# Opening stage of a four-layer vision network on one core: whole-row loads, relative positions by raster rows, key bias on chip, and paced expert weights

## The chip, the cores and the metric

The kernel runs on 1 core of a Trainium2 chip, in one launch. The time is device microseconds, the median of 3 runs. TensorE (PE) multiplies matrices into PSUM banks, VectorE (DVE), ScalarE (ACT) and GpSimd (POOL) do elementwise work, and SyncE (SP) mostly issues DMA transfers. The engines run side by side and wait for each other by semaphores.

## The reference, cut to what matters

The network has a window-attention block with an MLP, a Fourier block, a landmark attention, a two-expert layer, a full attention and a one-expert layer. Two places are touched: the front of the first block, and the last layer.

```python
h = _ln(x, norm1_w, norm1_b)             # x: 8 images of 16 x 16 tokens, 192 channels
win = windows(pad(h), 14)                # 14 x 14 windows; the real tokens give pieces of 14x14, 14x2, 2x14, 2x2
q, k, v = split(win @ qkv_w + qkv_b)     # 12 heads of 16 channels
attn = einsum('bqc,bkc->bqk', q * scale, k)
rel_h = einsum('bhwc,hkc->bhwk', q, rel_pos_h[h - k + 13])   # one small table for each row h of a window
rel_w = einsum('bhwc,wkc->bhwk', q, rel_pos_w[w - k + 13])   # and one for each column w
attn = softmax(attn + rel_h + rel_w)
...
h = gelu(expert_inputs[e] @ w1[e] + b1[e])           # last layer: 8 experts of 256 slots
expert_outputs[e] = gelu(h @ w2[e] + b2[e])
```

A padded token of a window has the key `qkv_b` alone (the key bias), and the kernel needs that bias times the scale as three bf16 pieces whose sum is the fp32 value. Queries, keys and relative positions are split in the same way (`Pieces`: ACT makes the first piece at L252, DVE the rest at L264, ACT the second piece at L268, POOL the third at L272, SP stores them).

## The kernel before

Each engine has its own program, written out by hand in the order in which it runs; a stage ends when all engines meet. Two stages matter here.

**The opening, `opening` (L307 to L602).** It has two parts.

- The image loop, one image of 256 tokens after another. DVE takes the statistics (L154, L157) and normalizes (L182); PE turns the result (L192); ACT scales it by the norm weights on its way out of PSUM (L203, L204). PE projects queries and keys (L438) and values (L445, every other image also L453). ACT copies q and k out (L505), and both go through `Pieces` to DRAM. DVE adds the value bias (L585, L589). Tokens of an image stand in window order: 14x14 first, then the three border pieces.
- Four rounds of `relative` (L455 to L466), for two channel halves by two axes. In each round PE multiplies the queries of one window row (or column) with that row's table, 32 matmuls into five PSUM banks: four banks for the 14x14 piece with 112 columns a row, and the fifth for all border pieces (16 or 112 columns a row). ACT empties banks 0 and 2, DVE banks 1, 3 and 4 (`evacuate_rel`), into RHW. Then RHW goes through `Pieces` in two halves, three DMAs a half, to the DRAM tensor rd. Three buffers of pieces take turns.

The order on SP's queue: loads of x, the qkv weights W, biases, the two relative tables RT as twelve transposing loads of 4-byte elements (L370), the key bias pieces to DRAM (L373, after ACT and DVE made them from `qkb`), a zero fill and constants, a wait until the key bias has landed, six loads that spread it over 96 partitions (L379), then the stores of q and k image by image, twelve loads of the first attention group (L913), and the rd stores (L281). On ACT's queue: the identity, norm weights, biases, convolution taps and a reversed identity, each as a transposing load of 4-byte elements except the identities. PE's first work is the reversal of the taps (L470), then 12 warm-up matmuls on the identity (L473).

**The last layer, `experts_each` (L2716) with `AllExperts` (L2685).** POOL gathers each expert's tokens (L2748), then 16 gate columns (L2752), then scatters results (L2757) and gathers the tokens of expert e+4. PE turns the tokens (L2784), computes six groups of hidden units for two experts (L2798, L2801), turns the next two experts' tokens and computes both results (L2812). ACT applies gelu (L2838, L2846); DVE adds the bias (L2873) and combines (L2883). Before `experts_each` SP keeps the rows in xn and loads the weights of experts 0 and 1; at its start, after PE's second turn, it issues the weights of experts 2 and 3, a store of all rows to `out`, and the weights of experts 4 to 7, without further waits. POOL's first scatter waits for that store.

Of the kernel before, what the change touches and what calls it, by code (L numbers as in the profile page):

```python
# [17 lines left out]
T = HH * WW  # L18
# [288 lines left out]
def opening(nc, G, x, w, w_conv, consts):  # L307

    with Stage(nc, "l0q") as st:
# [6 lines left out]
        taps, rev, backwards = st.sb("taps", [TAPS, NH]), st.sb("rev", [TAPS, TAPS]), st.sb("backwards", [NH, TAPS])  # L316
        wn, bn, qkb, kb4 = st.sb("wn", [CH, 2]), st.sb("bn", [CH, 2]), st.sb("qkb", [CH, 6]), st.sb("kb4", [CH, 2])
        kbp, kbr, kb = st.sb("kbp", [CH, 3, 2], BF16), st.sb("kbr", [CH, 2]), st.sb("kb", [SR, NH], BF16)
# [8 lines left out]
        ident_in, w_in, b_in, vb_in, tables_in, taps_in, band_out, first_in, kb_in, kb_out = st.sems("ident_in w_in b_in vb_in tables_in taps_in band_out first_in kb_in kb_out")  # L327
        rev_mm, rev_done, q_mm, q_free, k_mm, k_free, v_mm, v_free, e_free = st.sems("rev_mm rev_done q_mm q_free k_mm k_free v_mm v_free e_free")
        kb_step, kf_free, v_init, rbd_done, ones_done, pads_done = st.sems("kb_step kf_free v_init rbd_done ones_done pads_done")
        ps = [psE, nm.psT[0], nm.psT[1], psQ, psK]  # L330
        full, emptied = [st.sem(f"full{c}") for c in range(5)], [st.sem(f"emptied{c}") for c in range(5)]
# [3 lines left out]
        def fills(axis):  # L335

            first, *rest = runs(axis)
            out = [[(0, first, i0, min(4, WS - i0))] for i0 in range(0, WS, 4)]
            col, last = 0, []
            for run in rest:  # L340
                last.append((col, run, 0, run[0]))
                col += run[0] * B * run[3]
            return out + [last]

        def evacuate_rel(copy, bank, axis):
            for col, (n, base, si, cnt, step, su), i0, ni in fills(axis)[bank]:
                src = ps[bank][0:ROWS, col:col + ni * B * cnt].rearrange("p (i b u c) -> p i b u c", i=ni, b=B // 2, u=2)
                for u in range(2):
                    dst = RHW[:, axis, base + si * i0 + u * su:base + si * i0 + u * su + 1]
                    ins = copy(free(dst, [si, ni], [2 * T, B // 2], [step, cnt]), src[:, :, :, u])  # L350
            return ins
# [5 lines left out]
        def _(sp):  # L357
# [8 lines left out]
            sp.dma_start(vb[:, :], rows(w["qkv_b"], 2 * C, [0, P], [1, C])).then_inc(vb_in, 16)  # L366
            sp.dma_start(pb[:, :], rows(w["proj_b"], 0, [0, P], [1, C])).then_inc(vb_in, 16)
            for k, table in enumerate((w["rel_pos_h"], w["rel_pos_w"])):
                for hh in range(HB):
                    sp.dma_start(RT[hh * HD:(hh + 1) * HD, k, :], rows(table, 0, [1, HD], [HD, 2 * WS - 1]), allow_slow_non_contiguous=True).then_inc(tables_in, 16)  # L370
            sp.dma_start(hm[:, :], consts["headmask"]).then_inc(tables_in, 16)
            sp.wait_ge(kb_step, 5)
            sp.dma_start(rows(G["kbd"], 0, [1, CH], [2 * CH, 3], [CH, 2]), kbp[:, :, :], allow_slow_non_contiguous=True).then_inc(kb_out, 16)  # L373
# [3 lines left out]
            sp.wait_ge(kb_out, 16)  # L377
            for t, piece in enumerate(K_TERM):
                sp.dma_start(kb[t * HD:(t + 1) * HD, :], rows(G["kbd"], piece * C, [1, HD], [HD, NH]), allow_slow_non_contiguous=True).then_inc(kb_in, 16)  # L379
            for i in range(B):  # L380
                for pieces, dst in ((qp, G["qd"]), (kp, G["kd"])):
                    pieces.sync(sp, rows(dst, i // 2 * 3 * C * 2 * T + i % 2 * T, [2 * T, CH], [2 * C * T, 3], [2 * CH * T, 2], [1, T]), i, i % 2)
                if i == 0:
# [12 lines left out]
            sp.wait_ge(first_in, 16 * 14)  # L396
# [3 lines left out]
        def _(pool):  # L400
# [19 lines left out]
            for r, a, axis in rounds:  # L420
# [6 lines left out]
        def _(pe):  # L427
# [28 lines left out]
            def relative(r, a, axis):  # L456
                for bank, fill in enumerate(fills(axis)):
                    if r:
                        pe.wait_ge(emptied[bank], r)
                    else:  # L460
                        pe.wait_ge(*((e_free, B // 2), (nm.xT_done, B + 2), (nm.xT_done, B + 2), (q_free, B), (k_free, B))[bank])
                    for col, (n, base, si, cnt, step, su), i0, ni in fill:
                        for k in range(ni):
                            src = QF[:, a, base + si * (i0 + k):base + si * (i0 + k) + 1]
                            mm = nc.tensor.matmul(ps[bank][0:ROWS, col + k * B * cnt:col + (k + 1) * B * cnt], Rbd[:, axis, i0 + k, :],
                                                  free(src, [2 * T, B // 2], [su, 2], [step, cnt]), start=True, stop=True)  # L466
                    mm.then_inc(full[bank], 1)

            pe.wait_ge(taps_in, 32)
            nc.tensor.matmul(psR[0:NH, 0:TAPS], taps[:, :], rev[:, :], start=True, stop=True).then_inc(rev_mm, 1)  # L470
            pe.wait_ge(ident_in, 16)
            for _ in range(12):
# [4 lines left out]
            for i in range(B):  # L477
                project(i)
                if i % 2 == 0:
                    border(i // 2)  # L480
                if i + 2 < B:
                    nm.tensor(nc, pe, i + 2, i % 2)
            pe.wait_ge(rbd_done, 2)
            pe.wait_ge(q_free, B)
# [4 lines left out]
        def _(act):  # L489
            act.sem_inc(G["steady"], 1)  # L490
            act.dma_start(G["ident"][:, :], consts["ident"]).then_inc(ident_in, 16)
            act.dma_start(wn[:, :], w["norm1_w"].rearrange("(k p) -> p k", p=CH), allow_slow_non_contiguous=True).then_inc(b_in, 16)
            act.dma_start(bn[:, :], w["norm1_b"].rearrange("(k p) -> p k", p=CH), allow_slow_non_contiguous=True).then_inc(b_in, 16)
            act.dma_start(qkb[:, :], w["qkv_b"].rearrange("(m p) -> p m", p=CH), allow_slow_non_contiguous=True).then_inc(b_in, 16)
            act.dma_start(taps[:, :], rows(w_conv, 0, [1, TAPS], [TAPS, NH]), allow_slow_non_contiguous=True).then_inc(taps_in, 16)
            act.dma_start(rev[:, :], consts["reverse"]).then_inc(taps_in, 16)
            for pieces in (qp, kp, rp):
                pieces.init(act)
            act.wait_ge(b_in, 48)
# [14 lines left out]
            act.wait_ge(rev_mm, 1)  # L514
            nc.scalar.activation(backwards[:, :], psR[0:NH, 0:TAPS], ACT.Copy).then_inc(rev_done, 1)
            for i in range(B):
# [12 lines left out]
                seconds(i)  # L529
            for r, a, axis in rounds:  # L530
                if r >= 2:
                    act.wait_ge(rp.rest, FOURS * (r - 1))
                for bank in (0, 2):
                    act.wait_ge(full[bank], r + 1)
                    evacuate_rel(lambda o, i: nc.scalar.activation(o, i, ACT.Copy), bank, axis).then_inc(emptied[bank], 1)
                ready = [(emptied[bank], r + 1) for bank in range(5)]
# [7 lines left out]
        def _(dve):  # L544
# [7 lines left out]
            def rel_blocks(axis):  # L552
                if axis == 0:
                    dve.wait_ge(tables_in, 16 * (2 * HB + 1))
# [2650 lines left out]
```

## Time and profile before

| what | value |
|---|---|
| median of 3 runs | 1203.75 us (1201.72 to 1208.15) |
| the profiled execution's own time | 1209.1 us |
| its span, first to last instruction | 1207.2 us |
| mean granted TensorE clock | 0.891 |
| busy: PE, PE weight loads, DVE, ACT, POOL | 84%, 64%, 48%, 35%, 25% |
| the opening, in this span | 0 to 122.5 us |
| the last layer's experts | 1091.6 us to the end |

The busy shares are averages over many stages with different limits; what a change in one stage is worth is read from that stage's own waits and timeline. PE and PE weight loads overlap. A granted clock of 1.00 is TensorE's higher level and 0.50 its lower one.

### The profile page before, as it was taken

To read this page: it belongs to the slowest core of one execution; us is meant where nothing else is said; L and a number is where in the kernel's file an instruction comes from. 1 tells how busy PE (TensorE), PEld (TensorE's weight loads), DVE (VectorE), ACT (ScalarE), POOL (GpSimd) and SP (SyncE) were. 2 spreads that over 40 slices of the span, in tenths; PEclk is the share of its full clock that TensorE was granted. 3 is DMA by queue.
4 is the path that set the end of the run, shared out by engine and by line. 5 is a ranking of instruction groups with operands and counts; after the bars stand their busy time and mean duration, and the time that the engine had idled before them with its cause. 6 is when DMAs were issued, how large, how long until landed. Compare 5 with 4: busy or idle time off the path is not lost. (4 is left out here: it accounts for less than half of the span.)

```text
span 1207.2 us, 20472 instructions
## 1 busy us (share of the span) xinstructions
PE 1017.8 (84%) x7507; PEld 773.6 (64%) x7508; DVE 576.8 (48%) x1392; ACT 424.2 (35%) x858; POOL 298.7 (25%) x403
## 2 busy tenths in 40 slices
PE   6796999999798898999898459999487999864696
PEld 5696788886455686887797326666365455462575
DVE  4743555552211673564756634444376677331121
ACT  3564155555231332444440011111056366511232
POOL 4454310110110212000013035554222201106332
PEclk9875899999899898998887579999889999956798
DMA  8443753410011302000003511112144432056510
GB/s 87 114 129 105 167 137 83 104 47 2 1 63 56 76 4 54 1 1 1 2 1 104 192 34 49 48 49 49 32 140 106 127 107 81 2 203 203 222 42 14
DMA packets 103972, 91.70 MB, mean 76 GB/s; under 512 B 26416, under 2 KB 95749, under 8 KB 103244
## 3 DMA queue, kind: packets, MB, share of 16 engines
q1 hardware_dynamic: 91095, 75.68, 23.0%
q0 software_dynamic: 6144, 11.08, 3.5%
q10 hardware_dynamic: 6645, 3.75, 1.1%
q8 instruction: 57, 0.93, 0.4%
q14 instruction: 31, 0.25, 0.1%
HBM read 64.54 MB, written 29.70 MB: 78 GB/s over the span
## 5 line engine op out<-in xcount | busy, mean ns | idle before, releaser
L1224 DVE TENSOR_REDUCE l0a_nmax<-l0a_psS 98x2 f32<-98x392 f32 x96 | 54.4, 567 | 54.8 <-PE l0a_psS L1039 50.7
L868 DVE TENSOR_REDUCE l3a_nmax<-l3a_psS 128x2 f32<-128x512 f32 x96 | 62.0, 686 | 31.6 <-PE l3a_psS L722 31.6
L2642 ACT ACTIVATE l2e_H<-l2e_psH 128x512 f32<-128x512 f32 x40 | 21.7, 595 | 129.6 <-PE l2e_psH L2604 129.6
L824 ACT ACTIVATE l3a_PT<-l3a_psST 128x512 f32<-128x512 f32 x96 | 54.7, 597 | 28.7 <-PE l3a_psST L752 28.1
L2622 PEld LDWEIGHTS l2e_psY<-W2T,l2e_HT 128*128 128x128 f32 x320 | 51.5, 190 | 16.7 <-issue 16.6
L1174 ACT ACTIVATE l0a_PT<-l0a_psST 98x392 f32<-98x392 f32 x96 | 47.3, 498 | 42.1 <-PE l0a_psST L1081 41.7
L2566 POOL DMA_INDIRECT ys<-l2e_Y,result_of x40 | 42.3, 1058 | 71.4 <-DVE l2e_Y L2669 65.3
L2622 PE MATMUL l2e_psY<-W2T,l2e_HT 128*128 x320 | 57.3, 332 | 2.1 <-DVE l2e_Y L2669 0.8
L2561 POOL DMA_INDIRECT l2e_X<-xn,token_at x40 | 39.3, 983 | 59.0 <-PEq L2583 47.1
L2601 PE MATMUL l2e_psH<-W1T,l2e_XT 128*128 x80 | 41.0, 636 | 2.7 <-issue 2.0
L2798 PE MATMUL l3e_psH<-l3e_XT,l3w_A 128*128 128x256 f32 x96 | 30.2, 442 | 15.2 <-ACT l3e_HT L2838 10.9
L2669 DVE COPY l2e_Y<-l2e_psY 128x384 f32<-128x384 f32 x20 | 11.2, 558 | 64.9 <-PE l2e_psY L2622 63.0
L722 PE MATMUL l3a_psS<-l3a_KS,l3a_QS 96*128 96x256 bf16 x192 | 37.2, 275 | 3.0 <-DMA l3a_KS<-kd 2.3
L752 PE MATMUL l3a_psST<-l3a_QS,l3a_KS 99*128 99x256 bf16 x192 | 36.6, 273 | 0.5 <-ACT l3a_PT L824 0.3
L1400 DVE TENSOR_TENSOR X<-l0m_psY,X 128x384 f32<-128x384 f32 x8 | 4.5, 558 | 65.8 <-PE l0m_psY L1347 65.8
L1347 PE MATMUL l0m_psY<-early,l0m_hT 128*128 128x192 f32 x192 | 32.3, 328 | 2.4 <-ACT l0m_hT L1372 2.4
L2798 PEld LDWEIGHTS l3e_psH<-l3e_XT,l3w_A 128*128 128x128 f32 x96 | 18.5, 212 | 24.5 <-ACT l3e_HT L2838 11.6
L1347 PEld LDWEIGHTS l0m_psY<-early,l0m_hT 128*128 128x128 f32 x192 | 31.1, 190 | 3.9 <-ACT l0m_hT L1372 3.9
L1176 ACT ACTIVATE l0a_PT<-l0a_psST 120x360 f32<-120x360 f32 x48 | 22.2, 471 | 31.7 <-PE l0a_psST L1089 29.2
L2838 ACT ACTIVATE l3e_HT<-l3e_psH,l3w_A 128x256 f32<-128x256 f32 x48 | 19.9, 472 | 37.3 <-remote 18.7
L1227 DVE TENSOR_REDUCE l0a_nmax<-l0a_psS 120x1 f32<-120x312 f32 x48 | 22.9, 480 | 20.6 <-PE l0a_psS L1048 19.0
L1006 POOL CAST l0a_mp<-l0a_nmax 128x20 bf16<-128x20 f32 x12 | 2.4, 201 | 119.7 <-DVE l0a_nmax L1227 119.7
(545 smaller groups left out, 2746.3 us busy)
## 6 DMA issues: line engine op xcount, KB each, us to landing
l3w_A<-in_w SPq DMA_DIRECT2D x8, 771.0 KB, 12.5
l3w_B<-in_w SPq DMA_DIRECT2D x8, 672.0 KB, 13.5
l3a_QS<-qd SPq DMA_DIRECT2D x72, 64.0 KB, 2.3
l3a_KS<-kd SPq DMA_DIRECT2D x72, 64.0 KB, 2.3
rd<-l0q_r_p SPq DMA_DIRECT2D x24, 168.0 KB
l0a_QS<-qd SPq DMA_DIRECT2D x54, 64.0 KB
l0a_KS<-kd SPq DMA_DIRECT2D x54, 64.0 KB
W2T<-in_w2t SPq DMA_DIRECT2D x2, 1536.0 KB, 16.2
```

The source lines that it names most:

```text
L722: mm = nc.tensor.matmul(psS[item % 2][:, t * T:(t + 1) * T], QS[k % ring][0:SR, s, q:q + P], KS[k % ring][0:SR, s, u * T:(u + 1) * T], sta ...
L752: mm = nc.tensor.matmul(psST[item % 2][:, t * T:(t + 1) * T], KS[k % ring][:, s, key:key + P], QS[k % ring][:, s, u * T:(u + 1) * T], star ...
L824: nc.scalar.activation(PT[n % 3][:, s, :], psST[item % 2][:, :], ACT.Exp).then_inc(exp_done, 1)
L868: nc.vector.tensor_reduce(nmax[k % 2][:, TI * u:TI * (u + 1), s], psS[item % 2][:, :].rearrange("p (t k) -> p t k", t=TI), AX.X, ALU.max, ...
L1174: ex = nc.scalar.activation(PT[n % 3][0:WQ, s, :], psST[item % 2][0:WQ, 0:2 * W0], ACT.Exp)
L1224: mx = nc.vector.tensor_reduce(nmax[k % 2][0:WQ, 2 * j:2 * (j + 1), s], psS[item % 2][0:WQ, 0:2 * W0].rearrange("p (t k) -> p t k", t=2), ...
L1347: mm = nc.tensor.matmul(psY[a][:, t % 2 * C:(t % 2 + 1) * C], hT[p % 2][:, m, t * P:(t + 1) * P], Wd[:, m, :], start=(m == 0), stop=(m == ...
L2561: pool.indirect_dma_start(out=X[p % RING][:, t, :], out_offset=None, in_=G["xn"], in_offset=at(G["token_at"], 2 * p + t)).then_inc(x_in[p ...
L2566: pool.indirect_dma_start(out=G["ys"], out_offset=at(G["result_of"], 2 * p + t), in_=Y[p % RING][:, t, :], in_offset=None, bounds_check=2 ...
L2601: nc.tensor.matmul(psH[b][t][:, :], XT[b][:, t, :], W1T[:, 0, bass.ds(e * FI, FI)], start=True, stop=False)
L2622: mm = nc.tensor.matmul(psY[:, t * C:(t + 1) * C], HT[b][t][:, mb, :], W2T[:, bass.ds(e * NM + mb, 1), :].rearrange("p a c -> p (a c)"), s ...
L2798: nc.tensor.matmul(bank[h][:, 0:CAP], W1[e][:, 0, m * P:(m + 1) * P], XT[b][:, 0, :], start=True, stop=False)
```

## The change

- Small loads: the host lays out norm weights and q/k biases as one [96, 8] table (`cols`), taps and reversal as one table, the relative tables already transposed and repeated per head, and the key bias already spread over 96 partitions with a mask of pieces (`kbt`). Each is loaded by one DMA with whole rows per partition. `vb` is loaded before images 2 to 7. The taps' matmul goes behind the first image's projections; warm-up matmuls become 8.
- Key bias: `key_bias` on DVE, after image 5, makes the pieces in nine short instructions; the trip through DRAM and SP's wait for it are gone. The copy into KP now reads fp32.
- Relative positions: after each image's q is copied out, DVE copies it into raster order (`lines`, four copies, into QL). PE then takes whole raster rows or columns of 16 tokens for 8 images, 128 columns a matmul, 16 matmuls a round in four banks; rounds alternate between two sets of four banks. A bank's columns are sorted back into window order when it is emptied (four copies a bank, eight in the last bank). DVE makes the last round's third pieces in place of POOL.
- Experts: the store to `out` is issued before any expert weights. From expert 2 on, each expert's first weights wait for the first hidden group of the expert two earlier, and its second weights for the last one.

```diff
         @block.sync
             load(0); load(1); W
+            sp.dma_start(vb[:, :], rows(w["qkv_b"], 2 * C, [0, P], [1, C])).then_inc(vb_in, 16)
             for i in range(2, B):
                 load(i)
...
-            for k, table in enumerate((w["rel_pos_h"], w["rel_pos_w"])):
-                for hh in range(HB):
-                    sp.dma_start(RT[hh * HD:(hh + 1) * HD, k, :], rows(table, 0, [1, HD], [HD, 2 * WS - 1]), ...)
+            sp.dma_start(RT[:, :, :], w["tables"]).then_inc(tables_in, 16)
...
-            sp.wait_ge(kb_step, 5)
-            sp.dma_start(rows(G["kbd"], 0, [1, CH], [2 * CH, 3], [CH, 2]), kbp[:, :, :], ...).then_inc(kb_out, 16)
...
-            sp.wait_ge(kb_out, 16)
-            for t, piece in enumerate(K_TERM):
-                sp.dma_start(kb[t * HD:(t + 1) * HD, :], rows(G["kbd"], piece * C, [1, HD], [HD, NH]), ...).then_inc(kb_in, 16)
...
         @block.tensor
             def relative(r, a, axis):
+                for bank in range(4):
+                    ... # rounds 0 and 1: the bank's last reader of the image loop
+                        pe.wait_ge(emptied[r % 2][bank], r // 2)
+                    for k in range(LINES):
+                        i0 = LINES * bank + k
+                        src = QL[:, a, :, i0, :] if axis == 0 else QL[:, a, :, :, i0]
+                        mm = nc.tensor.matmul(ps[r % 2][bank][0:ROWS, k * B * WW:(k + 1) * B * WW], Rbd[:, axis, i0 % WS, :], src, ...)
+                    mm.then_inc(full[r % 2][bank], 1)
...
-            pe.wait_ge(taps_in, 32)
-            nc.tensor.matmul(psR[0:NH, 0:TAPS], taps[:, :], rev[:, :], ...).then_inc(rev_mm, 1)
             pe.wait_ge(ident_in, 16)
-            for _ in range(12):
+            for _ in range(8):
...
         @block.vector
+            def lines(i):
+                dve.wait_ge(q_free, i + 1)
+                for r0, c0, h, wd, n0 in WINDOWS:
+                    at = i * T + n0 + (i % 2) * (apart(n0) - T)
+                    cp = nc.vector.tensor_copy(QL[:, :, i, r0:r0 + h, c0:c0 + wd], QF[:, :, at:at + h * wd].rearrange(...))
+                cp.then_inc(raster, 1)
...
             for i in range(B):
                 norm(i + 2), stat(i + 4)
+                lines(i)
                 qp.vector(...); kp.vector(...)
...
                 if i == 5:
-                    dve.wait_ge(kb_in, 16 * len(K_TERM))
-                    nc.vector.tensor_copy(KP[0:SR, :, :], ...)
+                    key_bias()
...
 class AllExperts:
     def sync(self, sp):
         sp.dma_start(<xn>, self.G["X"][:, :, :]).then_inc(self.x_kept, 16)
-        self.load(sp, 0, 2)
+        sp.dma_start(<out>, self.G["X"][:, :, :]).then_inc(self.x_out, 16)
+        for e in range(2):
+            self.load_first(sp, e)
+            self.load_second(sp, e)
...
 def experts_each(nc, G, weights, out):
-            sp.wait_ge(xt_mm, 2)
-            weights.load(sp, 2, 4)
-            weights.keep_rows(sp)
-            weights.load(sp, 4, E)
+            for e in range(2, E):
+                sp.wait_ge(h_mm, H3 * (e - 2) + 1)
+                weights.load_first(sp, e)
+                sp.wait_ge(h_mm, H3 * (e - 1))
+                weights.load_second(sp, e)
```

## Rows read from the trace of the kernel before

**Rows 1.** Waits of all engines, 0 to 125 us (total us, times, longest).

```profile
PE l0q_psR L470 <- DMA l0q_rev<-const_reverse: 11.0, 1, 11.0
ACT l0q_q_p L252 <- DMA qd<-l0q_q_p: 8.1, 2, 7.0
```

**Rows 2.** Waits of SP's own queue, 0 to 125 us (total us, times, longest).

```profile
SPq L379 <- DMA kbd<-l0q_kbp: 13.9, 1, 13.9
SPq L397 <- DMA rd<-l0q_r_p: 1.9, 1, 1.9
```

**Rows 3.** Timeline: start us, length us, engine line operation xcount [idle before <-releaser].

```profile
6.27 0.67 DVE L182 TENSOR_SCALAR l0q_xn<-X,MV,RSTD 128x192 f32<-128x192 f32 x2 [0.37 <-POOL RSTD L163]
11.24 5.18 PE L473 MATMUL l0q_psE<-ident 128*128 128x128 f32 x24
18.11 1.94 PE L438 MATMUL l0q_psQ<-l0q_xT,early 96*96 96x256 f32 x8 [0.82 <-ACT l0q_xT L204]
35.03 1.89 PE L438 MATMUL l0q_psQ<-l0q_xT,early 96*96 96x256 f32 x8
46.85 3.49 PE L438 MATMUL l0q_psQ<-l0q_xT,early 96*96 96x256 f32 x8
71.69 0.93 PE L465 MATMUL l0q_psE<-QF,l0q_Rbd 96*84 96x112 f32 x8
```

**Rows 4.** Busy time by stretch and engine (instructions), granted clock, DMA share, GB/s.

```profile
core 0: us, PE busy (x) PEld busy (x) DVE busy (x) ACT busy (x) POOL busy (x), PEclk, DMA share, GB/s
41.00:71.00 30.00, 23.40 (x112) 18.74 (x113) 23.28 (x31) 21.94 (x48) 16.92 (x12) 0.89 0.45 112
71.00:123.00 52.00, 37.92 (x262) 37.80 (x260) 20.07 (x51) 24.48 (x38) 23.41 (x12) 0.56 0.39 114
```

**Rows 5.** The experts: waits, 1090 to 1207 us.

```profile
ACT l3e_HT L2838 <- remote: 18.7, 2, 13.2
```

**Rows 6.** The experts: timeline.

```profile
1108.50 0.70 PE L2801 MATMUL l3e_psH<-l3e_XT,l3w_A 64*128 64x256 f32 x4
...
1121.53 0.95 POOL L2752 DMA_INDIRECT l3e_gate<-gate_rows,token_at  x1 [0.30 <-issue]
...
1132.10 7.98 PE L2812 MATMUL l3e_psY<-l3w_B,l3e_HT 128*128 128x192 f32 x48
...
1137.85 1.02 POOL L2757 DMA_INDIRECT out<-l3e_R,result_at  x1 [15.37 <-DVE l3e_R L2883]
...
1151.39 0.66 PE L2784 MATMUL l3e_psX<-ident,l3e_X 128*128 128x128 f32 x4 [0.77 <-DMA l3e_X<-xn,token_at]
```

**Rows 7.** DMA issues, 0 to 125 us: count, KB each, median us to landing.

```profile
ident<-const_ident ACTq DMA_DIRECT2D x1, 64.0 KB, 3.2
```

**Rows 8.** The same normalization with POOL idle and beside POOL (timeline).

```profile
25.36 0.66 DVE L182 TENSOR_SCALAR l0q_xn<-X,MV,RSTD 128x192 f32<-128x192 f32 x2
...
58.69 2.30 DVE L182 TENSOR_SCALAR l0q_xn<-X,MV,RSTD 128x192 f32<-128x192 f32 x2
```

**Rows 9.** Instruction groups by shape, 0 to 160 us: count | busy us, mean ns.

```profile
L465 PE MATMUL l0q_psK<-QF,l0q_Rbd 96*84 96x16 f32 x128 | 16.4, 279 | 0.0
L272 POOL TENSOR_TENSOR l0q_r_p<-early,l0q_r_p 84x1024 bf16<-84x1024 f32 x6 | 12.7, 2126 | 14.5 <-ACT l0q_r_p L268 14.5
L252 ACT ACTIVATE l0q_r_p<-l0q_RHW 84x1024 bf16<-84x1024 f32 x8 | 8.1, 1052 | 17.4 <-DVE l0q_RHW L350 17.4
L264 DVE TENSOR_TENSOR early<-l0q_RHW,l0q_r_p 84x1024 f32<-84x1024 f32 x6 | 7.1, 1216 | 3.8 <-ACT l0q_r_p L252 3.8
L350 DVE COPY l0q_RHW<-l0q_psT 84x224 f32<-84x224 f32 x8 | 3.2, 463 | 0.0
L594 DVE COPY first_KP<-l0q_kb 96x2880 bf16<-96x2880 bf16 x1 | 1.6, 1645 | 0.0
L350 DVE COPY l0q_RHW<-l0q_psK 84x16 f32<-84x16 f32 x8 | 0.9, 159 | 0.0
```

**Rows 10.** The stores of rd: count: ns of an issue (least, median, most), first and last start.

```profile
L281 SPq DMA_DIRECT2D rd<-l0q_r_p x24: 764/772/870, 85.7 to 119.8; - x24
```

More of the change, by code:

```diff
@@ L304, in runs, with opening @@
         yield (h, n0, w, w, 1, apart(n0)) if axis == 0 else (w, n0, 1, h, w, apart(n0))
-def opening(nc, G, x, w, w_conv, consts):
+def opening(nc, G, x, w, consts):
     with Stage(nc, "l0q") as st:
@@ L332, in opening, with evacuate_rel @@
         rounds = [(2 * a + axis, a, axis) for a in range(2) for axis in range(2)]
         block = st.block()
[L335 to L347, printed above, removed]
+        def evacuate_rel(copy, s, bank, axis):
+            src = ps[s][bank][0:ROWS, 0:LINES * B * WW].rearrange("p (i b u c) -> p i b u c", i=LINES, b=B // 2, u=2)
+            for r0, c0, h, wd, n0 in WINDOWS:
+                along, across, n, m = (r0, c0, h, wd) if axis == 0 else (c0, r0, wd, h)
+                step_n, step_m = (wd, 1) if axis == 0 else (1, wd)
+                lo, hi = max(along, LINES * bank), min(along + n, LINES * (bank + 1))
+                if lo >= hi:
+                    continue
@@ L348, in evacuate_rel @@
                 for u in range(2):
-                    dst = RHW[:, axis, base + si * i0 + u * su:base + si * i0 + u * su + 1]
-                    ins = copy(free(dst, [si, ni], [2 * T, B // 2], [step, cnt]), src[:, :, :, u])
+                    at = n0 + step_n * (lo - along) + u * apart(n0)
+                    dst = free(RHW[:, axis, at:at + 1], [step_n, hi - lo], [2 * T, B // 2], [step_m, m])
+                    ins = copy(dst, src[:, lo - LINES * bank:hi - LINES * bank, :, u, across:across + m])
@@ L419, in _ @@
             nc.gpsimd.memset(KP[SR:QR, :, :], 1.0).then_inc(ones_done, 1)
-            for r, a, axis in rounds:
+            for r, a, axis in rounds[:-1]:
                 for u in range(FOURS):
@@ L480, in _ @@
                     border(i // 2)
+                if i == 0:
+                    pe.wait_ge(taps_in, 16)
+                    nc.tensor.matmul(psR[0:NH, 0:TAPS], taprev[:, 0:NH], taprev[:, NH:], start=True, stop=True).then_inc(rev_mm, 1)
                 if i + 2 < B:
@@ L533, in _ @@
                 for bank in (0, 2):
-                    act.wait_ge(full[bank], r + 1)
-                    evacuate_rel(lambda o, i: nc.scalar.activation(o, i, ACT.Copy), bank, axis).then_inc(emptied[bank], 1)
-                ready = [(emptied[bank], r + 1) for bank in range(5)]
+                    act.wait_ge(full[s][bank], r // 2 + 1)
+                    evacuate_rel(lambda o, i: nc.scalar.activation(o, i, ACT.Copy), s, bank, axis).then_inc(emptied[s][bank], 1)
+                ready = [(emptied[s][bank], r // 2 + 1) for bank in range(4)]
                 for u in range(FOURS):
```

131 lines of the change are left out of this document (74 added, 57 removed).

## The prediction

> **What bounds the kernel now.** The waits of the opening come first. The reader is to see two of them: PE begins only when the last small load has landed, 11.0 us in, and ACT once waits 7.0 us for the store of the first image's q [rows 1]. SP's own waits say why that store is late: SP stood 13.9 us until the key bias, sent to DRAM in 2-byte elements, had landed [rows 2]. The timeline puts both in place. The first projection starts at 18.11. Images then follow every 5.64 us ((35.03 - 18.11) / 3), but between the fourth and the fifth lie 11.82 us, and the fifth runs its 8 passes in 3.49 us where the fourth took 1.89 [rows 3]. The relative positions begin at 71.69. By stretches, PE is busy 23.40 of 30 us in the later images and DVE 23.28, so DVE has little to spare; from 71 to 123 us no engine is full but PE, and PE only because its granted clock is 0.56, mostly the lower (1.2 GHz) of its two levels [rows 4]. After the last store of rd SP waits 1.9 us [rows 2]; the opening ends at 122.5.
>
> Some 970 us follow that the edits do not enter. In the experts ACT waits twice, 18.7 us together, for something that the profile can't name [rows 5], while PE had finished the fourth of six groups at 1109.2 and its first results start only at 1132.10 [rows 6].
>
> **Start: -8.5 us.** The loads become rows, and PE no longer waits for the taps. The identity, issued at about 0.8, lands 3.2 us later [rows 7], so warm-up can start near 4.5 (an estimate). 24 passes took 5.18 us [rows 3], 8 matmuls are 16 passes, 3.5 us: 8.0. The normalized image is there at 6.94 (6.27 + 0.67 [rows 3]), so it is not late. From the end of warm-up (16.42) to the first projection took 1.69 us; the same again gives 9.65, against 18.11. At best the projection follows the normalized image: 6.94 + 1.69 = 8.6. At worst the small tables still land with the rest at 11.2: 12.9. Fewer warm-up passes may leave TensorE at its lower level: at 3.49 for 1.89 us a group of 8 passes, three such groups would lose 5 us. I take 9.65. W and images 2 to 7 have fewer descriptors ahead of them, so they are costed at nothing.
>
> **The key-bias stall: -7.8 us.** The store to DRAM and the six loads go; 11.82 becomes 5.64 (-6.2), and the fifth image keeps the higher clock (-1.6). What is late next is PE itself, which had no idle time in the first three images.
>
> **What DVE gets: +4.5 us.** `lines` is four copies of 392, 56, 56 and 8 elements. No row has such a copy between SBUF tiles; the nearest are the copies out of PSUM, 0.463 us for 224 elements and 0.159 for 16 [rows 9], which is 1.46 ns an element: 0.71 + 0.22 + 0.22 + 0.15 = 1.3 us an image. The normalization, two instructions of 192 elements, takes 0.66 us alone and 2.30 beside POOL's third pieces [rows 8], so a copy lies between 0.2 and 1.15, an image between 0.8 and 4.6 us. In the later images DVE is idle 22% of 5.64, 1.25 us an image [rows 4], and `lines` stands where DVE would wait for ACT's first piece anyway. Queued behind it are the rests of q and k, for which ACT's second pieces wait, and later the next normalization, for which PE waits. I take 1.3, mostly hidden, and +2.5 for images 4 to 6, where the table blocks also lie. `key_bias` adds eight chained instructions at about 0.2 us, and the copy into KP reads 4-byte elements: 1.65 us [rows 9] becomes perhaps 3. That is 3 us more on DVE at image 5; the last normalization is done by then, so I take +2. Bounds: 0 (all in idle time) to (4.6 - 1.25) x 8 + 3 = +30 us.
>
> The Trainium skill (SBUF — State Buffer, Who interferes with whom) speaks against these copies: a DVE copy between SBUF tiles can enter a mode that takes the port pair shared with GpSimd for a whole instruction, and the other engine then blocks; who issues first wins. The two normalization rows agree with it. By that rule, with every copy blocked, this term would be near its upper bound, the fourth rival below.
>
> **Rounds of relative positions: -5.5 us.** Before, a round is 32 matmuls, among them 16 of 16 columns whose 128 passes in all fill 16.4 us [rows 9]; one bank set makes PE wait until ACT and DVE have emptied it. After, 16 matmuls of 128 columns, 32 passes a round, and the next round's banks are free: 4.3 us a round at the higher level, 7.5 at the lower, from 0.116 us a pass of 112 columns (0.93 / 8 [rows 3]). PE is then ahead, and the chain goes over ACT, DVE, POOL, SP and the three piece buffers. Emptying two banks costs ACT some 2.5 us (four of 224 elements, four of 32), DVE 3 (its last bank has eight copies). Then come a first piece 1.05, rest 1.22, second 1.05, third 2.13 on POOL [rows 9], three issues of 0.77 [rows 10] and 1.9 to land. Counted from PE's first relative matmul, SP is free for rd only at +14.0 as before (85.7 - 71.7), behind the q and k stores and the twelve loads of the first group. So piece 0 lands at +18.3 (14.0 + 2.3 + 1.9), and the fourth piece, which needs its buffer, waits for that although its data are there at +14: the new wait, and ACT's second piece of the third one is queued behind it. From there: third piece's POOL part done +22.7, landed +26.9, which releases the sixth piece; round 3's eighth piece waits for the fifth (+35.4), and after rest, second piece and DVE's third (1.22, for POOL's 2.13) SP issues the last three at +41.3 to +43.6 and they land at +45.5. Before: 122.5 - 71.7 = 50.8. Bounds: if buffers never bind, ACT alone needs 4 x (2.5 + 4.2) plus the tail, +40; if the new copies are twice as long, +51.
>
> Sum of the opening: -8.5 - 7.8 + 4.5 - 5.5 = -17.3 us.
>
> **Experts: -10 us.** SP issues the weights of six experts and the store to `out` in one go, and ACT's two waits fall in the time in which they land [rows 5]. Paced, at most one expert's load is in flight behind a group. PE would go on from 1109.2 with two more groups and two turns, and start results near 1116, 16 us sooner. But not all of that is kept: POOL issues the last gate until 1122.48 [rows 6], DVE's first combination needs all gates, hence comes no sooner than about 1124.5 (1.9 us to land, as for rd), and with 1.5 us to combine and issue (an estimate) the first scatter goes out at 1126.0 instead of 1137.85 [rows 6]. From there to the second turned pair took 13.5 us (1151.39 - 1137.85), two scatters and two gathers twice; that chain now stands at 1139.5: -11.9. PE's part up to there (results 8 us [rows 6], two hidden layers some 10) is done near 1135, so it idles 4 us and may fall to the lower clock: +2. Late next is thus POOL, not the weights: expert 4's come 18 us before their use. The store to `out` now runs before experts 0 and 1, in a routing stage that waits for other things; it is costed at nothing there. Bounds: 0 (the wait has another cause) to -13.
>
> The Trainium skill (SBUF — State Buffer, Who interferes with whom) says that DMA never contends with a compute engine. By that rule ACT's waits can't come from the loads, and this term would be 0: the first rival. The rows leave it open, for the wait has no name in them.
>
> **Sum.** 1209.1 (this execution's own time) - 17.3 - 10 = 1181.8. The median of the runs shown lies 5.35 us under this execution; of that I keep 5, since a part may be a longer stall in the experts that goes in any case: 1177.
>
> **Rivals.**
> - Pacing gains nothing; the unnamed wait is not the loads' doing. For it: PE and ACT show no such wait in the routing stage under experts 0 and 1. Against: both waits end while loads are landing. 1177 + 10 = 1187. Chance 0.15.
> - DVE sets the pace of the image loop: with 78% busy before and 1.3 us more an image, plus gaps for ACT, each image takes 1.2 us more. 1177 + 9 = 1186. Chance 0.10.
> - The loads don't do what they say: rows or not, they land behind x and W, and the projection starts at 12.9 or later, partly at the lower clock: 1177 + 8 = 1185. Chance 0.06.
> - Slower: every copy of `lines` waits out both of POOL's subtractions, 2.30 us each as the pair of normalizations did, 9.2 an image. Less 1.25 idle that is +8 x 8 = 64 us in the image loop, against 31.8 gained elsewhere (8.5 + 7.8 + 5.5 + 10): 1204 + 32 = 1236. It decides from 5.3 us an image on. For it: the later normalizations all show 2.3. Against: POOL works 2.3 us an image in the third pieces, and four copies can't all meet them. Chance 0.03.
> - The buffers don't bind: SP reaches rd sooner, and the rounds end at +40: 1171. Chance 0.08.
>
> **How the numbers follow.** The forecast has 0.58. The likeliest case alone spans 1172 to 1182; with the rivals on either side I give 1168 to 1191, which leaves the slower rival and mixtures of two bad ones outside. About 0.5%, 6 us, is what a measurement of this kernel can tell from no change. Faster by more: forecast, three rivals that still gain 17 or more, and the buffers' case, less mixtures, 0.94; within: 0.03; slower: 0.03.
>
> **What would show it.** First projection near 9.7 and images every 5.6 to 6.3 us without a gap; no SP wait on the key bias; PE's relative matmuls within 20 us of their start, ACT waiting for rd stores before the fourth piece; opening over near 105; no unnamed ACT wait in the experts, and PE waiting 4 us for gathered tokens before its second pair of turns. The prediction is wrong if DVE's copies show over 2 us an image, if the fifth image still lags, or if ACT's unnamed wait stays.

## The result and the profile after

The changed kernel takes 1191.84 us (median of 4, 1189.95 to 1195.85) against 1205.12 us for the kernel before beside it (1201.72 to 1208.15): ratio 0.9904, 95% interval 0.988 to 0.9928. It is faster by 13.3 us where the forecast's 1177 us would have been 28.1 faster, and it lies just over the upper end of the range (1191). The profiled execution takes 1192.1 us, 17.0 less than the one profiled before (1209.1).

The opening went as forecast. Timeline of the changed kernel (start us, length us, engine, line, operation [idle before <- releaser]); each Q row is an image, L461 is the first relative matmul, and the last row opens the attention stage:

```profile
4.23 3.78 PE L466 MATMUL l0q_psE<-ident 128*128 128x128 f32 x16 [4.23 <-DMA ident<-const_ident]
10.12 1.94 PE L432 MATMUL l0q_psQ<-l0q_xT,early 96*96 96x256 f32 x8 [0.77 <-ACT l0q_xT L204]
27.34 1.89 PE L432 MATMUL l0q_psQ<-l0q_xT,early 96*96 96x256 f32 x8
32.53 1.89 PE L432 MATMUL l0q_psQ<-l0q_xT,early 96*96 96x256 f32 x8
58.42 1.94 PE L461 MATMUL l0q_psT<-l0q_QL,l0q_Rbd 96*84 96x128 f32 x15 [1.62 <-issue]
105.06 0.30 ACTq L1188 DMA_DIRECT2D l0a_RS<-const_winrows  x1
```

The row of before that answers to the last one:

```profile
123.00 0.28 ACTq L1164 DMA_DIRECT2D l0a_RS<-const_winrows  x1
```

PE starts its warm-up when the identity lands, and its first projection at 10.12 in place of 18.11 [rows 3]. The fifth image follows the fourth by 5.19 us where there were 11.82, and its 8 passes take 1.89 us, not 3.49 [rows 3]. (The fourth starts at 27.34, the fifth at 32.53.) Waits of the changed kernel, 0 to 105 us (total us, times, longest); SP has none on the key bias any more [rows 2]:

```profile
ACT l0q_r_p L252 <- DMA rd<-l0q_r_p: 8.4, 3, 3.6
```

That is the new wait that the forecast named: the pieces of the relative positions wait for a buffer.

The experts did not go as forecast. ACT's operations of the first pair, POOL's first and last gather of gates, its first scatter, and the last turn of tokens that PE makes during the second pair of experts, in the changed kernel ("remote" is a releaser that the profile can't name):

```profile
1090.33 0.84 ACT L2864 ACTIVATE l3e_HT<-l3e_psH,l3w_A 128x256 f32<-128x256 f32 x2
1091.63 0.84 ACT L2864 ACTIVATE l3e_HT<-l3e_psH,l3w_A 128x256 f32<-128x256 f32 x2 [0.46 <-issue]
1096.18 0.84 ACT L2864 ACTIVATE l3e_HT<-l3e_psH,l3w_A 128x256 f32<-128x256 f32 x2 [3.71 <-PE l3e_psH L2827]
1105.40 0.84 ACT L2864 ACTIVATE l3e_HT<-l3e_psH,l3w_A 128x256 f32<-128x256 f32 x2 [8.38 <-remote]
1111.67 1.57 ACT L2864 ACTIVATE l3e_HT<-l3e_psH,l3w_A 128x256 f32<-128x256 f32 x4 [5.44 <-remote]
...
1088.22 0.94 POOL L2778 DMA_INDIRECT l3e_gate<-gate_rows,token_at  x1 [0.30 <-issue]
1106.94 0.94 POOL L2778 DMA_INDIRECT l3e_gate<-gate_rows,token_at  x1 [0.30 <-issue]
1117.00 1.02 POOL L2783 DMA_INDIRECT out<-l3e_R,result_at  x1 [9.12 <-DVE l3e_R L2909]
...
1132.24 0.66 PE L2810 MATMUL l3e_psX<-ident,l3e_X 128*128 128x128 f32 x4 [1.99 <-DMA l3e_X<-xn,token_at]
```

ACT's waits of 3.71, 8.38 and 5.44 us are still there, though only one expert's weights are in flight. The waits end as the 16 gathers do, in both kernels: the last gather ends at 1107.88 and the last wait at 1111.67; before, 1122.48 [rows 6] and 1126.29:

```profile
1126.29 1.57 ACT L2838 ACTIVATE l3e_HT<-l3e_psH,l3w_A 128x256 f32<-128x256 f32 x4 [13.25 <-remote]
```

And SP, which now counts PE's groups too, sees the same late counts. Timeline of its queue:

```profile
1088.99 0.33 SPq L2735 DMA_DIRECT2D l3w_A<-in_w  x1
1096.17 0.33 SPq L2738 DMA_DIRECT2D l3w_B<-in_w  x1
1105.33 0.33 SPq L2735 DMA_DIRECT2D l3w_A<-in_w  x1
1111.76 0.33 SPq L2738 DMA_DIRECT2D l3w_B<-in_w  x1
```

So it is PE's report of a finished group that comes late, to both engines that wait for it. The last matmuls of the third and fourth groups by PE's own records:

```profile
1092.58 0.70 PE L2827 MATMUL l3e_psH<-l3e_XT,l3w_A 64*128 64x256 f32 x4
...
1094.27 0.70 PE L2827 MATMUL l3e_psH<-l3e_XT,l3w_A 64*128 64x256 f32 x4
```

They are over at 1093.28 and 1094.97 (by ends that the profile models); ACT and SP go on at 1096.2 and 1105.3. In the other direction nothing is late: PE's next group starts at 1106.29, 0.05 us after ACT's operation of 1105.40 ends.

### The profile page after: what moved, and what is told of

It reads as the page before. It is cut to its first block and busy times, and to the rows that moved or that the text cites. A ratio compares the mean times of both kernels' runs of the same rounds, so it can differ in the third digit from the quotient of the medians.

```text
span 1190.3 us, 20238 instructions
## 1 busy us (share of the span) xinstructions
PE 1008.4 (85%) x7371; PEld 760.1 (64%) x7372; DVE 586.6 (49%) x1438; ACT 424.3 (36%) x874; POOL 294.1 (25%) x401
## 5 line engine op out<-in xcount | busy, mean ns | idle before, releaser
L2838 PE MATMUL l3e_psY<-l3w_B,l3e_HT 128*128 128x192 f32 x192 | 32.0, 327 | 0.0
```

The costliest lines, as they stand in the source:

```text
L2838: mm = nc.tensor.matmul(psY[t][:, 0:C], HT[b][:, m, t * P:(t + 1) * P], W2[e][:, m, :], start=(m == 0), stop=(m == MF - 1))
```

## Experiments

Two theories of that stall were set against each other, G (the gathers of gates) and W (the weight loads, the forecast's). From the rows of POOL, the spans that matter, in us: from the first fetch of tokens to the first scatter (the stall is in it), between the first scatters of successive pairs of experts, and from the first fetch to the end.

| kernel | to first scatter | 2nd pair | 3rd | 4th | to the end |
|---|---|---|---|---|---|
| before | 45.24 | 19.67 | 19.32 | 17.92 | 114.65 |
| changed | 38.94 | 21.36 | 21.55 | 17.93 | 112.20 |
| a1, changed again | 43.35 | 21.93 | 23.21 | 17.92 | 118.86 |
| e1, unpaced | 45.31 | 19.30 | 19.30 | 17.93 | 114.26 |
| e2, no gathers of gates | 26.86 | 26.54 | 20.99 | 17.92 | 103.15 |
| e3, e1 and e2 | 26.14 | 19.73 | 19.16 | 17.93 | 93.77 |
| e4, gathers spread | 27.71 | 23.21 | 23.11 | 17.96 | 104.38 |
| e7, e4 unpaced | 27.62 | 21.72 | 21.76 | 18.06 | 101.54 |
| e8, gates on chip, unpaced | 26.56 | 19.64 | 19.24 | 17.92 | 94.08 |
| e9, wide gathers | 38.29 | 20.57 | 21.44 | 17.92 | 110.66 |
| e10, one by one | 40.07 | 28.42 | 27.42 | 17.70 | 124.47 |
| e12, before, gates on chip | 27.43 | 22.78 | 19.30 | 17.92 | 98.26 |
| e13, gathers of 16 rows | 45.74 | 25.89 | 23.46 | 17.92 | 125.45 |
| e14, POOL busy | 26.94 | 23.21 | 21.55 | 17.92 | 100.74 |
| e5, changed, four buffers | 39.51 | 21.13 | 23.25 | 17.93 | 114.28 |
| e11, e8 with four buffers | 26.68 | 19.94 | 19.33 | 17.92 | 94.64 |

**a1_after** is the changed kernel once more. 

> The changed kernel once more, as the yardstick for the runs beside it. Every theory expects the time of its first measurement, 1190 to 1196 us, some 13 us under the kernel before, and in the experts stage again ACT waits of about 3.7, 8.4 and 5.4 us that end in the stretch of the 16 gate gathers.

Measured: 1197.08 us against 1210.75, ratio 0.988 (0.9847 to 0.9913). The time lies 1 us above the 1190 to 1196 expected. ACT waits 5.96, 11.21 and 1.27 us: the stall is there, of another size. In the first profile, here and in e5, whose experts are the same, the first scatter comes after 38.94, 43.35 and 39.51 us, so one profile can differ from the next by 4 us.

**e1_unpaced**

```diff
-            for e in range(2, E):
-                sp.wait_ge(h_mm, H3 * (e - 2) + 1)
-                weights.load_first(sp, e)
-                sp.wait_ge(h_mm, H3 * (e - 1))
-                weights.load_second(sp, e)
+            sp.wait_ge(xt_mm, 2)
+            for e in range(2, E):
+                weights.load_first(sp, e)
+                weights.load_second(sp, e)
```

> The changed kernel with the experts' weights loaded as before: all twelve from the third expert's on as soon as two pairs are turned, none paced. Theory G (the 16 gathers of gate values hold up what PE reports to ACT and SP): the stall of the first experts lasts as long as the gathers, whatever the weights do; ACT's waits sum to 17 to 19 us again and the time stays within 3 us of the changed kernel. Theory W (the forecast's: the loads hold it up, and pacing them took some of it away): the first scatter comes some 10 us later behind its stage's start, and the time goes up by 2 to 10 us.

Measured: 1189.1 us, ratio 0.983 (0.9804 to 0.9855). Not slower than the paced kernel beside it, against what W expected; but 8 us faster, which G did not expect either. Of these, 6.3 lie ahead of the first fetch (1072.86 against 1079.13), in stages where the two kernels are the same: from the start of the first attention stage to the first fetch the profiles here differ by up to 8 us (967.3 to 975.1). Behind it ACT waits 9.65 and 9.10 us, and the first scatter is as late as before the change, 2.0 us later than in a1 and 6.4 later than in the first profile of the changed kernel. Loads alone cause no stall (e3, below); whether they lengthen the one that the gathers cause isn't shown, as e13, with paced loads, has 45.74. The later pairs are 2.6 and 3.9 us shorter than in a1. In the paced kernels PE waits for fetched tokens there (1.99 us at the second pair, above, and 2.40 in a1), while loads run beside the fetches; in e1 it has no such wait, and the loads are over before the fetches start.

**e2_no_gates**

```diff
+            nc.gpsimd.memset(gate[:, :], 1.0).then_inc(g_in, 16)
-            pool.wait_ge(weights.gate_kept, 16)
-            for e in range(E):
-                gates(e)
```

> The changed kernel without the 16 gathers of gate values (every gate is set to 1, so the weighting by the gates is left out); the weights are paced as in the change. Theory G: ACT's three unexplained waits (3.7, 8.4 and 5.4 us) shrink to under 2 us in all, the six groups of the first pair run at 1.9 to 3.3 us each, the first scatter comes 10 to 13 us earlier behind its stage's start, and the time goes down by 7 to 13 us against the changed kernel. Theory W: the waits stay, and the time is within 2 us of the changed kernel.

Measured: 1180.57 us, ratio 0.9765 (0.9742 to 0.9789), 16.5 under a1, where G expected 7 to 13; the stall of a1 was a long one. ACT's operations of the first pair without the gathers:

```profile
1083.90 0.84 ACT L2859 ACTIVATE l3e_HT<-l3e_psH,l3w_A 128x256 f32<-128x256 f32 x2
1085.15 0.84 ACT L2859 ACTIVATE l3e_HT<-l3e_psH,l3w_A 128x256 f32<-128x256 f32 x2 [0.41 <-PE l3e_psH L2822]
1086.85 0.84 ACT L2859 ACTIVATE l3e_HT<-l3e_psH,l3w_A 128x256 f32<-128x256 f32 x2 [0.85 <-PE l3e_psH L2822]
1088.60 0.84 ACT L2859 ACTIVATE l3e_HT<-l3e_psH,l3w_A 128x256 f32<-128x256 f32 x2 [0.91 <-PE l3e_psH L2822]
1090.23 0.84 ACT L2859 ACTIVATE l3e_HT<-l3e_psH,l3w_A 128x256 f32<-128x256 f32 x2 [0.79 <-PE l3e_psH L2822]
1091.93 0.84 ACT L2859 ACTIVATE l3e_HT<-l3e_psH,l3w_A 128x256 f32<-128x256 f32 x2 [0.85 <-PE l3e_psH L2822]
```

A group every 1.7 us and no stall, beside loads paced in the same way.

**e3_unpaced_no_gates** joins the two edits. 

> The changed kernel without the 16 gathers of gate values (gates set to 1, the weighting left out) and with the weights loaded as before, none paced. If the loads by themselves hold up the first pair (theory W), ACT's waits in the first six groups stay above 5 us in all although no gather is left. If only the gathers do (theory G), the six groups run at 1.7 us each as they did without gathers and with paced loads, and the first scatter comes 26 to 28 us after the first fetch. Then the later pairs, which with paced loads wait 2.2 to 4.9 us for fetched rows, don't wait, and follow at 19.3 us each: 4 to 8 us less than without gathers and with paced loads.

Measured: 1173.15 us, ratio 0.9723 (0.9677 to 0.9769). All loads at once and still no stall: ACT's waits between the groups are 0.80 to 1.14 us, so the loads by themselves don't cause it, and W is refuted. They land beside these groups at 354 GB/s (columns as in [rows 4]):

```profile
1089.00:1095.00 6.00, 5.42 (x27) 3.12 (x26) 0.00 (x0) 3.15 (x9) 0.00 (x0) 1.00 1.02 354
```

Waits of PE for fetched tokens in the experts (total us, times, longest), first e2 with paced loads, then e3:

```profile
PE l3e_psX L2805 <- DMA l3e_X<-xn,token_at: 14.2, 4, 6.7
```

```profile
PE l3e_psX L2804 <- DMA l3e_X<-xn,token_at: 8.8, 3, 6.7
```

Two pairs wait for tokens with paced loads that hardly wait without (4.91 and 1.43 us against 0.85 and none): the second pair comes after 26.54 and 19.73 us. It is not only that loads are there: in e3 they still land until about 1113, beside the fetches of 1105.83 to 1113.50. In e2 the loads of the second pair are issued among the fetches (1102.24 to 1110.71), and PE gets the last token 7.4 us after the issue of its fetch ended, in e3 3.3. Pacing costs here what the table shows, 9.4 us to the end (7.0 in e14, paced and without gathers too); the ratios' intervals overlap, so the size rests on the traces.

**e4_gates_spread** and **e7_spread_unpaced**

```diff
-            for e in range(E):
-                gates(e)
+            gates(0)
+            gates(1)
...
+                if e % 2 and e + 2 < E:
+                    gates(e + 1)
+                    gates(e + 2)
```

> The changed kernel with four of the 16 gathers of gate values where they are, and four more behind the scatters and row fetches of each pair of experts (12 gathers moved; each pair waits for its own gates alone). Theory G: the stall of the first pair shrinks to that of four gathers (5 us of them, 3 to 6 us of ACT's waits in place of 17), the moved gathers stall later groups by up to 3 us a time, and the time goes down by 4 to 9 us against the changed kernel. Theory W: the stall is the same, and the time is within 2 us of the changed kernel or above it by what 12 gathers of 1.25 us cost POOL between its scatters.

> The gathers of gate values spread over the pairs (four ahead of the first, four behind each pair's fetches) and the weights loaded as before, none paced. Theory G with the loads in the way of the fetches only: the later pairs follow at about 21 us (the four gathers still stall them, the fetches no longer wait), the whole 2 to 5 us below the spread gathers with paced loads. If pacing is good for anything once the gathers are spread: 2 to 5 us above it.

Measured: e4 1178.24 us, ratio 0.9732 (0.971 to 0.9755); e7 1180.1 us, 0.9784 (0.9735 to 0.9832), on another chip. The first pair is nearly free; the second and third, which now have four gathers beside them, are 2.0 and 2.6 us longer in e7 than in e3. There ACT's last three groups of the second pair come after waits of 2.01, 1.94 and 3.40 us. e7's last four gathers, for the fourth pair, follow four scatters and no fetch, and beside them ACT never waits more than 1.06 us. G expected 4 to 9 us of gain for e4; 18.8 against a1 is more, since a1's stall was a long one. Between paced and unpaced the traces say 2.8 us for unpaced, the times nothing.

**e12_before_gates_on_chip** and **e8_gates_on_chip** take the gates of each place out of the routing stage's one-hot matrices:

```diff
-                nc.tensor.transpose(psU[0:NT, 0:P], best[:, :], G["ident"][:, :]).then_inc(gate_mm, 1)
+                for k in range(2):
+                    for t in range(NT):
+                        mm = nc.tensor.matmul(psU[:, 0:TILES], OL[0][:, t, :], OHG[k][:, t, :], start=(k == 0 and t == 0), stop=(k == 1 and t == NT - 1))
...
+                link(V.tensor_copy(GP[0][:, :], best[:, :]))
+                link(V.tensor_tensor(GP[1][:, :], best[:, :], GP[0][:, :], ALU.subtract))
+                for k in range(2):
+                    ins = V.tensor_tensor(OHG[k][:], OH[:], free(GP[k][:, 0:1], [1, NT], [0, TILES]), ALU.mult)
```

> The gate of each place comes from the routing stage's own one-hot matrices (gate split in two 16-bit pieces, 32 more matmuls of 16 columns, four more VectorE operations) instead of a store and 16 gathers; weights not paced. Theory G: no stall in the first pair, 26 to 28 us from the first fetch to the first scatter, then 19.3 us a pair; the routing stage ends 0.5 to 2 us later; in all 8 to 14 us below the unpaced kernel with its gathers (ratio to the kernel before 0.97 to 0.975). Theory W: within 3 us of the unpaced kernel with gathers.

> The kernel before with one edit, the gates from the routing stage's own matrices in place of the 16 gathers; its opening and its unpaced weights are as they were. Theory G: its wait of 18.7 us at the experts goes, from the first fetch to the end it takes 94 to 97 us in place of 114.65, and the time is 16 to 21 us under the kernel before (ratio 0.983 to 0.987). Theory W, by which its unpaced loads are the cause: within 3 us of the kernel before.

Measured: e8 1173.44 us, ratio 0.9732 (0.9684 to 0.9779); e12 1191.3 us, 0.9854 (0.9817 to 0.9892). e12 answers by itself the question that the forecast got wrong: it has the opening and the unpaced loads of the kernel before, no gathers of gates, and no stall. ACT's operations of its first pair:

```profile
1104.24 1.57 ACT L2839 ACTIVATE l3e_HT<-l3e_psH,l3w_A 128x256 f32<-128x256 f32 x4
1106.94 0.84 ACT L2839 ACTIVATE l3e_HT<-l3e_psH,l3w_A 128x256 f32<-128x256 f32 x2 [1.14 <-PE l3e_psH L2802]
1108.69 0.84 ACT L2839 ACTIVATE l3e_HT<-l3e_psH,l3w_A 128x256 f32<-128x256 f32 x2 [0.91 <-PE l3e_psH L2802]
1110.33 0.84 ACT L2839 ACTIVATE l3e_HT<-l3e_psH,l3w_A 128x256 f32<-128x256 f32 x2 [0.80 <-PE l3e_psH L2802]
1112.02 0.84 ACT L2839 ACTIVATE l3e_HT<-l3e_psH,l3w_A 128x256 f32<-128x256 f32 x2 [0.85 <-PE l3e_psH L2802]
...
1119.41 1.02 POOL L2761 DMA_INDIRECT out<-l3e_R,result_at  x1 [17.57 <-DMA out<-X]
```

Its first scatter waits for the store to `out`, which before stands among the loads; the change's earlier store was worth about 1 us there. To the end the stage takes 98.3 us, a little over what was expected (94 to 97): its second pair takes 22.78 us where e8's takes 19.64, and PE waits 3.37 us for tokens there, in e8 0.22.

**What of a gather does it: e9, e13, e14, e10.** In e9 each gather brings 768 bytes a row, in e13 it brings 16 rows of 128, and in e14 memsets stand in its place:

```diff
-                    pool.indirect_dma_start(out=gate[:, t:t + 1], out_offset=None, in_=G["gate_rows"], in_offset=at(G["token_at"], t)).then_inc(g_in, 16)
+ e9                 pool.indirect_dma_start(out=spare[:, t, :], out_offset=None, in_=G["xr"], in_offset=at(G["token_at"], t)).then_inc(s_in, 16)
+ e13                pool.indirect_dma_start(out=spare[0:16, t:t + 1], out_offset=None, in_=G["gate_rows"],
+ e13                                        in_offset=bass.IndirectOffsetOnAxis(ap=G["token_at"][0:16, t:t + 1], axis=0)).then_inc(s_in, 16)
+ e14                nc.gpsimd.memset(spare[:, t, :], 0.0)
```

> The 16 gathers of 4 bytes a row replaced by 16 gathers of 768 bytes a row, of rows that nothing uses (gates set to 1, the weighting left out); the weights paced as in the change. If it is the 4-byte rows that hold up the reports of PE, the stall goes (ACT's waits in the first six groups under 6 us in all, the first scatter 27 to 31 us after the first fetch). If any gather issued by POOL beside these groups does it, the waits sum to 15 us or more and the first scatter comes 39 to 44 us after the first fetch.

> The changed kernel, and each of the 16 gathers of gate values brings 16 rows instead of 128 (gates set to 1, the weighting left out): the same 16 issues on POOL, an eighth of the rows. If the rows in flight are what holds up the reports of PE, the stall shrinks to under 6 us of ACT's waits in the first six groups and the first scatter comes 27 to 31 us after the first fetch, as without gathers. If each issue of a gather on POOL does it, whatever it brings, ACT's waits stay at 15 us or more and the first scatter at 38 to 44 us.

> The changed kernel with the 16 gathers of gate values replaced by 16 memsets of 640 elements on POOL into rows that nothing uses (gates set to 1, the weighting left out). If it is only that POOL is busy beside the groups, some stall is left (over 5 us of ACT's waits in the first six groups). If it needs a gather, there is none: waits of about 1 us a group, the first scatter 26 to 28 us after the first fetch, and the time that of the kernel without gate gathers, 15 to 18 us under the changed kernel.

Measured: e9 1189.83 us (ratio 0.9862, 0.9799 to 0.9925), e13 1200.5 (0.9921, 0.9877 to 0.9966), e14 1178.56 (0.9755, 0.972 to 0.979). e9's first scatter, after 38.29 us, lies just under the 39 to 44 expected; its waits (1.79, 8.32 and 7.53 us) sum to 17.6. ACT in e13, an eighth of the rows and the stall in full:

```profile
1086.15 1.61 ACT L2867 ACTIVATE l3e_HT<-l3e_psH,l3w_A 128x256 f32<-128x256 f32 x4
1097.47 0.84 ACT L2867 ACTIVATE l3e_HT<-l3e_psH,l3w_A 128x256 f32<-128x256 f32 x2 [9.70 <-remote]
1108.06 1.57 ACT L2867 ACTIVATE l3e_HT<-l3e_psH,l3w_A 128x256 f32<-128x256 f32 x4 [9.76 <-remote]
```

So the stall needs neither short rows nor many of them; it comes with the run of 16 gathers. Whether it is their issuing or that they are under way is not shown. The 16 memsets of e14 leave no stall (waits of at most 0.92 us), but they kept POOL busy for only 9.2 us, the gathers 20, so a POOL that is busy for as long with other work is not excluded.

**e10_one_by_one** is e7, and POOL waits for the fetches and then for each gather of gates to land. 

> The spread gathers with unpaced weights, and POOL waits until the fetches have landed and then for each gather of gate values before it issues the next. If a backlog of gathers that have not landed holds up the reports of PE, ACT's waits in all pairs fall to what they are without gathers (1 us a group, 2.1 at the longest) and the pairs follow at 19 to 20 us unless POOL is late with its scatters. If it is enough that POOL issues gathers beside the groups, the waits stay (2 to 3.4 us at some groups) and the pairs follow at 21.7 us or more.

Measured: 1201.49 us, ratio 0.9931 (0.991 to 0.9952). Inconclusive: ACT's first pair has waits of 0.80 to 1.14 us, but only one gather was issued beside it, and POOL, which waits 4.5 to 5.4 us for each gather there, is late with its scatters. A backlog is thus neither shown nor excluded.

**e5_four_buffers** and **e11_four_buffers_gates**, the second with e8's edits:

```diff
-        rp = Pieces(st, G, "r", ROWS, (1, FOUR * T), 3, 3, (rests["r0"], rests["r1"]))
+        rp = Pieces(st, G, "r", ROWS, (1, FOUR * T), 4, 3, (rests["r0"], rests["r1"]))
```

> The changed kernel with four buffers instead of three for the pieces of the relative positions in the opening. If ACT's waits for the stores of those pieces (3.58, 2.68 and 2.17 us) set the end of the opening, they shrink to under 3 us in all and the next stage starts 4 to 7 us sooner than at 105.06. If SyncE's 24 issues of 0.77 us or the arithmetic are next behind them, 0 to 3 us sooner.

> The changed kernel with the gates from the routing stage's matrices, the weights not paced, and four buffers in the opening: the gains of the two add, 18 to 25 us under the changed kernel, ratio to the kernel before 0.965 to 0.975.

Measured: e5 1184.41 us, ratio 0.9798 (0.9759 to 0.9838). Its waits for the stores of rd and the start of its attention stage:

```profile
ACT l0q_r_p L252 <- DMA rd<-l0q_r_p: 1.8, 2, 1.2
```

```profile
96.34 1.05 ACTq L1188 DMA_DIRECT2D l0a_RS<-const_winrows  x3
```

The opening ends 8.7 us sooner, more than the waits that went (6.6) and than the 4 to 7 expected. e11 takes 1163.35 us, ratio 0.9627 (0.9592 to 0.9663): the fastest kernel here, ahead of both.

## Why the prediction was wrong

The step that failed is "Experts: -10 us": ACT's unnamed wait was put on the loads of weights, and it belongs to the 16 gathers of gates. With it went a smaller one, the 5 us taken off for the median.

- **Start, -8.5.** 18.11 became 10.12: -8.0. Right.
- **Key-bias stall, -7.8, and DVE's additions, +4.5.** Together -3.3 to the first relative matmul; measured (58.42 - 10.12) - (71.69 - 18.11) = -5.3. The step from the fourth image to the fifth gives -6.6 of it (5.19 for 11.82), as forecast (-6.2). Ahead of the fourth image 0.3 us were lost. From the fifth on +1.1 was measured (25.89 us for 24.84), where +2.9 follows from the forecast (4.5, less 1.6 for the clock); the sixth and seventh images come 6.99 and 6.96 us after the ones ahead of them, over the 6.3 that was named. DVE's additions were priced too high. The copies of `lines`, forecast at 1.3 us an image, took 0.60 to 0.63 us in the five images in the middle and 1.49 to 2.76 us in the first two and the last, which run beside POOL's zero fill (12.53 to 15.62) and its third pieces (from 19.29 and 56.68). The Trainium skill (SBUF — State Buffer, Who interferes with whom) has such copies blocked on a port shared with GpSimd; a spread of 0.60 to 2.76 us for the same four copies agrees with it, but it held DVE up in three images only, so the slower rival did not come. DVE was busy 28.5 us of 30 from 28 to 58 us, near to setting the pace.
- **Rounds, -5.5.** (105.06 - 58.42) - (123.00 - 71.69) = -4.7, with the new wait where it was forecast. Right; the last rival's condition, that buffers don't bind, came nearly true in e5 (1.8 us of waits left; its rounds end at +38.6).
- **Sum of the opening, -17.3.** Measured -17.9. That it meets so well is in part luck: two of the gains came out smaller and one larger, and e12, with the opening of before, ends it at 121.00 and not 123.00.
- **Between the opening and the experts, 0.** Here 3.4 us were given back (first fetch 1078.06 against 1092.60, -14.5). Most of it is in the first attention stage, the same code, 188.3 us against 185.2. The opening is not the cause: in the other kernels with the new opening the stage took 184.2 to 188.3, and in e12, with the old one, 188.3. What differs between these two is the granted clock at the stage's end, where 2.9 of the 3.1 us lie. PE is busy 157 of the 158 us ahead of it in both and granted the upper level (2.4 GHz). In the changed kernel the clock then falls at about 282 us, inside the stage, and the first 8 matmuls of the last projection take 2.93 us; before, it holds until about 305, the end of the stage, and they take 1.57. Why it falls sooner in the one is not shown. Windows of the changed kernel (columns as in [rows 4]), then the same work before:

```profile
123.00:281.00 158.00, 156.99 (x2053) 126.38 (x2050) 82.08 (x181) 82.38 (x174) 21.71 (x57) 1.00 0.33 80
281.00:290.00 9.00, 6.92 (x25) 6.10 (x24) 1.79 (x5) 1.18 (x2) 0.00 (x0) 0.62 0.00 0
```

```profile
140.70:298.70 158.00, 157.00 (x2052) 126.36 (x2050) 82.10 (x181) 82.53 (x174) 21.81 (x57) 1.00 0.31 80
298.70:305.00 6.30, 3.94 (x24) 3.40 (x24) 2.02 (x6) 1.08 (x2) 0.00 (x0) 1.00 0.00 0
```

- **Experts, -10.** Measured -2.4 in the first profile (112.20 against 114.65), +4.2 in a1 (118.86) and -0.4 in e5 (114.28). Two things failed. The cause: ACT's unnamed wait was put on the weight loads because it falls in the time in which they land; the gathers of gates fall in the same time, and e3 and e12 show that it is theirs. The forecast named no way in which a load would hold up a group that PE had finished at 1109.2, 17 us before ACT's wait ended; that row [rows 6] already spoke against it. That the wait is not the loads' doing was the first rival, given 0.15, and its 1187 is the nearest of the prices. The Trainium skill's sentence behind it (SBUF — State Buffer, Who interferes with whom), that DMA never contends with a compute engine, agrees as far as the loads go: e3 has all of them and no stall. The gathers are DMA too, and how they hold up the reports is not shown. The price: pacing moved loads beside the fetches of later tokens, which cost 2 to 4 us in each of two pairs and was in no term; the 4 us that the forecast had PE wait there were not put on the loads.
- **The median, -5.** The profiled execution of before lay 4 us over its median in the end, that of the changed kernel 0.3. Most of the 5 us taken off for this should not have been.

From 1177: +7.6 for the experts, +3.4 in the middle, +4.7 for the median (0.3 kept of 5), -0.6 for the opening come to 1192.1; measured 1191.84. These are differences of two profiles, so they must add up; the size of the experts' share alone moves by some 7 us from one profile to the next.

## What to carry to other kernels

When a wait has no name, list everything that runs beside it, on every engine and queue, before it is given to the largest transfer: an experiment that takes one candidate away says more than that candidate's share of the bandwidth. Loads that are paced have to go somewhere, so look at which small transfers they will now meet. And where a forecast names the wait that comes next (here the third buffer), the next step is already written: one buffer more was worth as much (8.7 us) as the sooner start of the opening (8.0).

## What was not expected of the hardware

A run of 16 gathers issued by POOL beside short groups of matmuls holds up PE's reports. In the changed kernel ACT and SP saw the third group 2.9 us and the fourth 10.4 us after PE's own records end it. The stall comes with 4 or 768 bytes a row and with 128 or 16 rows. Twelve weight loads, 0.67 to 0.77 MB each, beside the same groups don't do it (e3). Shorter runs do less: beside the eight scatters and fetches of the second pair ACT's waits in e3 and e8 are 0.77 to 0.86 us at the first groups and 1.37 and 2.06 at the fourth, and with four gathers more (e7) they reach 3.40. Why a run of gathers does it is open.
